# A conv-attention, windowed-attention and expert kernel: the gate projection and the router as one token-major product

## The reference, cut to what matters

```python
# layer 1
t = t + windowed(_ln_t(t), Wp, bp, Wg)      # Wp 128x256, Wg 1x128
t = t + moe(_ln_t(t), router_w, w1, b1, w2, b2)

def windowed(x, Wp, bp, Wg):
    proj = tanh(einsum('btd,ad->bta', x, Wp) + bp)
    g = sigmoid(einsum('bta,oa->bto', proj, Wg))
    return windowed_sum(g * x, 64) / windowed_sum(g, 64)

def moe(tokens, router_w, ...):             # 8 experts, the best 2 of a token
    logits = tokens @ router_w.T
    ...
```

## Time and profile before

| | |
|---|---|
| median of 3 runs | 1453.36 us (1451.39 to 1463.06) |
| the profiled execution, its own time | 1452.11 us |
| its span, first to last instruction | 1450.2 us |
| mean granted TensorE clock | 0.954 of 2.4 GHz |
| busy in the span | PE 90%, DVE 78%, PEld 78%, ACT 68%, POOL 52% |

### The profile page before, as it was taken

One profiled execution on the slowest core, in us unless ns is written; L12 is line 12 of the kernel. 1 busy time (PEld: TensorE's weight loads), 2 busy tenths in 40 slices (PEclk: granted clock), 3 DMA queues, 4 the chain that ended last, 5 costly groups with the idle time before them and its releaser, 6 DMA issues. The chain is left out here.

```text
span 1450.2 us, 29384 instructions
## 1 busy us (share of the span) xinstructions
PE 1300.4 (90%) x8513; PEld 1132.8 (78%) x8513; DVE 1126.9 (78%) x3945; ACT 982.4 (68%) x2090; POOL 761.3 (52%) x964
## 2 busy tenths in 40 slices
PE   3899999989999999999999864999999999999974
PEld 3788878878778878788888743888879899998962
DVE  5478777778878778677778667788879899998972
ACT  1677667666667767667767553777778788888852
POOL 3114655646546565646565447355555556555560
PEclk9999999999999999999999966999999999999995
DMA  8622443535334122222211117766689999999978
GB/s 276 210 81 79 116 117 86 147 78 140 94 91 137 62 75 67 79 67 68 78 46 46 43 48 258 259 227 226 229 262 339 323 343 346 337 342 326 343 261 302
DMA packets 132524, 255.69 MB, mean 176 GB/s; under 512 B 41744, under 2 KB 54800, under 8 KB 132112
## 3 DMA queue, kind: packets, MB, share of 16 engines
q1 hardware_dynamic: 97744, 165.44, 36.2%
q0 software_dynamic: 25920, 71.60, 14.2%
q10 hardware_dynamic: 8704, 16.78, 3.0%
HBM read 120.14 MB, written 100.68 MB: 152 GB/s over the span
## 5 line engine op out<-in xcount | busy, mean ns | idle before, releaser
L1798 POOL DMA_INDIRECT answers<-yy,dest_i x284 | 289.3, 1019 | 223.0 <-DVE yy L1951 123.2
L1521 POOL DMA_INDIRECT sent<-tn,slot_s x256 | 275.9, 1078 | 146.7 <-issue 76.3
L1849 PE MATMUL s_bank<-band,hh 128*128 x568 | 165.8, 292 | 6.0 <-issue 2.9
L1498 POOL TENSOR_TENSOR rs<-ve,halves 128x4 f32<-128x4 f32 x64 | 64.9, 1019 | 195.7 <-DVE ve L1213 195.7
L791 PE MATMUL o_bank<-vv,at 128*128 128x256 f32 x512 | 144.2, 406 | 23.8 <-ACT at L981 14.8
L1849 PE MATMUL s_bank<-w_s,hh 128*128 x568 | 159.1, 280 | 0.5 <-issue 0.5
L1849 PE MATMUL s_bank<-band,hl 128*128 x568 | 158.8, 280 | 0.8 <-issue 0.8
L1933 ACT ACTIVATE zz<-xin 128x256 f32<-128x256 f32 x284 | 147.7, 600 | 10.2 <-issue 6.9
L1899 ACT ACTIVATE hid<-m_bank,b_all 128x512 f32<-128x512 f32 x142 | 93.0, 683 | 86.8 <-remote 60.2
L759 PE MATMUL m_bank<-wvo,band 128*128 128x258 f32 x792 | 135.1, 308 | 13.3 <-DVE band L1351 10.9
L759 PEld LDWEIGHTS m_bank<-wvo,band 128*128 128x128 f32 x792 | 109.5, 195 | 29.4 <-issue 27.7
(11 more groups left out here) (248 smaller groups left out, 3445.2 us busy)
## 6 DMA issues: line engine op xcount, KB each, us to landing
xin<-sent SPq DMA_DIRECT2D x71, 524.0 KB
got<-answers SPq DMA_DIRECT2D x64, 512.0 KB
w1hs<-rT SPq DMA_DIRECT2D x71, 256.0 KB
w1ls<-w_s SPq DMA_DIRECT2D x71, 256.0 KB
xs<-in_x SPq DMA_DIRECT2D x32, 512.0 KB, 8.2
raw<-in_x SPq DMA_DIRECT2D x32, 512.0 KB
out_x<-tn ACTq DMA_DIRECT2D x32, 512.0 KB
answers<-yy,dest_i POOLq DMA_INDIRECT x284
```

What stands on the lines that cost most here:

```text
L1498: eng.tensor_tensor(rs[:, n, :], ve[:, n, :], halves[:, 0, 0:KT], ALU.pow).then_inc(root.sem, 1)
L1521: eng.indirect_dma_start(sent, bass.IndirectOffsetOnAxis(slot_s[:, par, j, k:k + 1], 0), tn[:, par, k, :], None).then_inc(scattered[par], 16)
L1798: eng.indirect_dma_start(answers, bass.IndirectOffsetOnAxis(dest_i[:, at_ % RING, k:k + 1], 0), yy[:, slot, k, :], None).then_inc(rows_out ...
L1849: last = eng.matmul(y_bank[half][:, k * C:(k + 1) * C], hx[:, par, f, ts], rhs, start=(n == 0), stop=(n == 3 * CC - 1))
```

## The change

The router logits are no longer made from the second norm. The token row after the windowed attention is t + w/d, with w the sum of gated, normalized rows xn and d the sum of gates; the first norm's xn has mean zero, so the second norm's mean is the first's, and the router's product on (t - mean) is std * (xn R) + (sum of g * (xn R)) / d. So 8 columns xn R are made once, beside the gate projection, and ride along through the window sums as columns 256 to 263 of `xn1`, `wx` and `tt`.

- The gate projection is now token-major: for each tile `xn1T` is the stationary operand, and the moving one is `wpr`, 128 projection and 8 router columns. A pass with `onesr` and `bpr` puts the bias into the bank (its rounded and its remaining part). Two jobs, `Cp01` and `Cp23`, each with 2 x 136 columns, in place of `Cproj`.
- The product with `wg` is a dot product on VectorE (`dots`), four of 128 elements; `dots` also copies the router columns from the bank to `xn1`, and `routed_part` writes std * (xn R) to `tt`.
- `tokens_turned`, `tokens_taken`, `router` and `gates` are gone, with `tnT` and `logit`. `best_of` searches in `tt`; the difference of the best two is multiplied by the second norm's factor.
- The tanh comes in two halves. `gates_taken` waits for the dots. Banks are dealt out anew; `window(it, 0)` now stands behind the value product 3, and the copy `x_taken(it, 2)` ahead of the gates.

```diff
-        JOBS = ("VV0 AV1 AR0 Epos BX01 AR1 Dtr01 Dtr23 Ctr01 Ctr23 Drouter Cproj AV2 Cgate BX23 AV4 Cwin0 AV3 "
-                "Cwin1 Cwin2 Cwin3").split()
+        JOBS = ("VV0 AV1 AR0 Epos BX01 AR1 Ctr01 Ctr23 Cp01 Cp23 AV2 BX23 AV4 AV3 Cwin0 Cwin1 Cwin2 Cwin3").split()
...
+        bank_of["Cwin3"] = bank_of["Cwin0"]
...
+            eng.tensor_copy(onesr[:, :], ones[:, :])
+            eng.memset(bp_both[:, :, :], 0.0)
+            eng.tensor_copy(bp_high[:, :], bp_rows[:, :]).then_inc(biased, 1)
...
-            def gate_product(it):
-                moved(it, "Ctr01")
-                moved(it, "Ctr23")
-                bank = begin(it, "Cproj")
-                for cc in range(CC):
-                    last = eng.matmul(bank[:, :], wp_s[:, cc, :], xn1T[:, cc, :], start=(cc == 0),
-                                      stop=(cc == CC - 1))
-                end(last, "Cproj")
...
+            def gate_product(it, k0):
+                job = f"Cp{k0}{k0 + 1}"
+                moved(it, f"Ctr{k0}{k0 + 1}")
+                bank = begin(it, job)
+                eng.matmul(bank[:, 0:2 * PR], onesr[:, :], bpr[:, :, :].rearrange(flat), start=True, stop=False)
+                for k in (k0, k0 + 1):
                     for cc in range(CC):
...
+                        last = eng.matmul(bank[:, (k - k0) * PR:(k - k0 + 1) * PR], xn1T[:, cc, k * P:(k + 1) * P],
+                                          wpr[:, cc, :], start=False, stop=(k > k0 and cc == CC - 1))
...
-                if d:
-                    tokens_turned(it, 0)
-                    tokens_turned(it, 2)
...
-                eng.scalar_tensor_tensor(row, m_bank[i][:, 0:C], wden[:, k:k + 1], row, ALU.mult, ALU.add)\
+                eng.scalar_tensor_tensor(row, m_bank[i][:, 0:C + E], wden[:, k:k + 1], row, ALU.mult, ALU.add)\
                    .then_inc(taken[i].sem, 1)
 
+            def dots(it, k0):
+                i = bank_of[f"Cp{k0}{k0 + 1}"]
+                th_ready.wait(eng, it, f"Cth{k0}{k0 + 1}")
...
+                for k in (k0, k0 + 1):
+                    last = eng.tensor_tensor_reduce(out=th[:, k, :], in0=th[:, k, :], in1=wg_rows[:, :], scale=1.0,
+                                                    scalar=0.0, op0=ALU.mult, op1=ALU.add, accum_out=gl[:, k:k + 1])
+                if k0 == 2:
+                    last.then_inc(gate_step.sem, 1)
+                eng.tensor_copy(xn1[:, k0:k0 + 2, C:C + E],
+                                m_bank[i][:, 0:2 * PR].rearrange("p (k n) -> p k n", k=2)[:, :, A:PR])\
+                   .then_inc(taken[i].sem, 1)
+
+            def routed_part(it):
+                for job in ("Cp01", "Cp23"):
+                    taken[bank_of[job]].wait(eng, it, job)
+                done(gate_step, eng.tensor_tensor(tt[:, it.block("C") % TT, :, C:C + E], xn1[:, :, C:C + E],
+                                                  std1[:, :].unsqueeze(2).broadcast_to([P, KT, E]), ALU.mult))
...
+                step(it, route, "Dgap", eng.tensor_tensor(fall[:, :], best[:, :, 1], best[:, :, 0], ALU.subtract))
+                root.wait(eng, it, "Drs2")
+                done(route, eng.tensor_tensor(fall[:, :], fall[:, :], rs[:, 1, :], ALU.mult))
```

More of the change, by code:

```diff
@@ L323, in group_variance @@
                 eng.wait_ge(g_sum, 2)
-            eng.tensor_scalar(g2[:, :], bank[:, 96:96 + CC], EPS, None, ALU.add).then_inc(scale_step, 1)
+            eng.tensor_scalar(g2[:, :], bank[:, 320:320 + CC], EPS, None, ALU.add).then_inc(scale_step, 1)
         def group_root(eng, img, n):
@@ L519, in prologue_vector @@
             eng.tensor_copy(band_prev[:, :], prev_s[:, :])
+            eng.tensor_copy(onesr[:, :], ones[:, :])
+            eng.memset(bp_both[:, :, :], 0.0)
+            eng.tensor_copy(bp_high[:, :], bp_rows[:, :]).then_inc(biased, 1)
+            eng.wait_ge(biased, 1)
+            eng.tensor_tensor(bp_low[:, :], bp_rows[:, :], bp_high[:, :].bitcast(f32), ALU.subtract)\
+               .then_inc(biased, 1)
+            eng.wait_ge(biased, 2)
+            eng.tensor_scalar(bp_low[:, :], bp_low[:, :], ident[:, 1:2], None, ALU.mult).then_inc(biased, 1)
+            eng.wait_ge(biased, 3)
+            for n in range(2):
+                last = eng.scalar_tensor_tensor(bp_both[:, n, 0:A], bp_high[:, :].bitcast(f32), ident[:, 0:1],
+                                                bp_low[:, :], ALU.mult, ALU.add)
+            last.then_inc(biased, 1)
+            eng.wait_ge(biased, 4)
+            eng.tensor_copy(bpr[:, :, :], bp_both[:, :, :])
             eng.tensor_copy(far2[:, 0:REAL].rearrange("p (a b) -> p a b", b=W), far[:, :, 1:W + 1])
@@ L826, in window @@
                 for h in range(2):
-                    last = eng.matmul(bank[:, 0:C + 2], band_cur[:, :], wx[:, par, h, k, :], start=(h == 0),
+                    last = eng.matmul(bank[:, 0:XC], band_cur[:, :], wx[:, par, h, k, :], start=(h == 0),
                                       stop=(alone and h == 1))
@@ L844, in gates @@
-            def gates(it):
-                moved(it, "Cproj")
-                bank = begin(it, "Cgate")
-                for k in range(KT):
-                    last = eng.matmul(bank[:, k:k + 1], pT[:, k * P:(k + 1) * P], wg_s[:, :], start=True,
-                                      stop=True)
-                end(last, "Cgate")
-            def router(it):
-                moved(it, "Dtr01")
-                moved(it, "Dtr23")
-                bank = begin(it, "Drouter")
-                for k in range(KT):
-                    for cc in range(CC):
-                        last = eng.matmul(bank[:, k * E:(k + 1) * E], tnT[:, cc, k * P:(k + 1) * P],
-                                          rw_s[:, cc, :], start=(cc == 0), stop=(cc == CC - 1))
-                for n in range(2):
-                    if image_of(it, 6 - n):
-                        last = group_product(eng, image_of(it, 6 - n), n, bank)
-                end(last, "Drouter")
+            def gate_product(it, k0):
[4 more added lines that the diff above has]
+                for k in (k0, k0 + 1):
+                    for cc in range(CC):
+                        last = eng.matmul(bank[:, (k - k0) * PR:(k - k0 + 1) * PR], xn1T[:, cc, k * P:(k + 1) * P],
+                                          wpr[:, cc, :], start=False, stop=(k > k0 and cc == CC - 1))
+                if k0 == 0:
+                    for n in range(2):
+                        if image_of(it, 6 - n):
+                            last = group_product(eng, image_of(it, 6 - n), n, bank)
+                end(last, job)
@@ L942, in body @@
                 if c:
+                    window(it, 0)
                     window(it, 1)
@@ L1305, in best_of @@
             def best_of(it):
-                i = bank_of["Drouter"]
-                full[i].wait(eng, it, "Drouter")
-                if image_of(it, 6):
-                    group_spread(eng, image_of(it, 6), m_bank[i])
-                if image_of(it, 5):
-                    group_variance(eng, image_of(it, 5), m_bank[i])
-                eng.tensor_copy(logit[:, :, :].rearrange(flat), m_bank[i][:, 0:KT * E])\
-                   .then_inc(taken[i].sem, 1)
-                alone(eng, (taken[i].sem, taken[i].count(it, "Drouter")))
+                scores = tt[:, it.block("D") % TT, :, C:C + E]
                 for k in range(KT):
-                    last = eng.max(best[:, k, :], logit[:, k, :])
+                    last = eng.max(best[:, k, :], scores[:, k, :])
                 last.then_inc(route.sem, 1)
@@ L1431, in body @@
                     band_lower(it)
+                if c:
+                    dots(it, 0)
+                    dots(it, 2)
+                    routed_part(it)
                 if d:
```

124 lines of the change are left out of this document (65 added, 59 removed).

## The result

The changed kernel takes 1483.1 us (median of 4 runs, 1474.2 to 1488.4), the kernel before 1452.4 on the same chip (1449.5 to 1463.1): a ratio of 1.019, 95% interval 1.015 to 1.024. It is slower, by 1.5 to 2.4%, where I had forecast 1419. Both numbers have to be explained.

The account below looks back on a forecast made before the run. TensorE bounds clean rounds now, VectorE (21.8 us a round) after. 1452.1 - 34.5 (rounds) - 3 (hand-over) + 0.5 (start) + 3 (clock) = 1418, with the runs' median 1419 us; range 1403 to 1436.

Parts of the forecast that it names:

- the round after: Walk through one changed round: gates open only 0.4 us earlier, later waits shrink, giving 22.4 us, or 23.15 with statistics.
- the 0.78 wait: VectorE's wait for a window sum in a clean round, 0.78 us, expected to shrink after the change.
- TensorE's lag before the last weighing: TensorE's lateness past the gates, ahead of a round's last weighing; expected to shrink, with no separate size.
- stalls whose cause the trace doesn't name: With the clock, the excess of rounds over 23.95 us, 1.4 in first and 0.7 in later ones; expected to stay.
- The clock: In the thirty rounds, two more low-clock stretches were expected after the change, adding 3 us.
- rival (c): Clock falls in one stretch a round: 22 more stretches give back 40 us, total 1456; chance 0.06.
- (d): Clock falls twice a round, from idleness ahead of fourth value product and third weighing: slower, 1509; chance 0.06.
- stand next to idleness: Claim that today's low-clock stretches in the rounds, some 3.5 us each, lie beside TensorE idle time, such as 3.15 us.
- the hand-over: The 59 us between rounds and expert tiles: search waits and slower router passes go, saving 3 us.
- the sixteen with statistics: Rounds 2 to 17, where VectorE also takes a later image's statistics: 23.15 us each, saving 12.8 together.
- the missing wait at the search: VectorE's 2.03 us wait for the router's product, ahead of the search of the best two experts, goes.
- The idleness ahead of the fourth value product: New TensorE wait for a bank, until the first two dots and their copy are done; no separate size.

Follow-up runs that it names:

- b_same: The kernel before with nothing changed, profiled on a chip without the hold: 1385.8 us (one run).
- a_same: The changed kernel with nothing else changed, on a chip without the hold: 1339.8 us against 1385.1 for the kernel before, 0.966.
- b_split: The kernel before with GpSimd's eight sends of a round issued in two halves of four: 1384.6 us, 0.999 of the kernel before.
- b_nosend: The kernel before with GpSimd's eight indirect sends of a round left out: 1379.8 us, 0.996 of the kernel before.
- b_light: The kernel before without the normalized tokens' transposes and copies, two router passes in place of sixteen, nothing added on VectorE: 1331.8 us, 0.963.
- chip 9: The one experiment chip with the hold; the kernel before takes 1451.6 us there (7 runs).
- b_hold_fill8: b_hold plus eight useless matmuls of 128 columns on TensorE ahead of the fourth weighing, on chip 9: 1495.9 us, 1.031 of the kernel before.
- a_split_6: The changed kernel with a round's eight sends in two halves of four, on chip 9: 1383.0 us (one run), 4.7% less than the kernel before.
- a_hold: The changed kernel with second window sum and last transposed attention read only after all eight sends landed: 1502.1 us, 1.087 of the kernel before.
- b_hold: The kernel before with the same two waits for the sends as a_hold: 1495.7 us, 1.081 of the kernel before.

## Why the prediction was wrong

**The step that failed** is in the round after: "past them the 0.78 wait and TensorE's lag before the last weighing shrink". I had read the 0.78 us ahead of VectorE's window sum as TensorE being late. It was the end of a hold: TensorE starts the last matmul of that sum at 666.95 and its event comes 0.95 us later, not 0.30; the wait isn't there in b_same, and its clean rounds are 23.0 to 23.2 us long, not 23.96. So was, by its place and size, at least part of the "stalls whose cause the trace doesn't name": all 27 jobs that are held for over 2 us lie in rounds of 25.5 us or more. The waits of the kernel before had the sign in them, ten of VectorE ahead of a window sum (total, times, longest), and I didn't ask what "remote" was:

```profile
DVE wden L1288 <- remote: 20.3, 10, 2.7
```

In the changed kernel they didn't shrink: VectorE's wait for the window sum became 1.74 us, and TensorE idles for 1.66 us ahead of the last weighing, behind a wait of 3.24 of ScalarE. It is not that it puts more of TensorE's work into the sends: between 3 and 10 us after a round's first send it starts 7.6 jobs a round, the kernel before 8.1. The hold sets in earlier. Of the jobs in that stretch that can be paired 128 of 172 take over 0.8 us in the changed kernel, 44 of 150 in the kernel before. Why is open.

The account in the rounds, hold against no hold: +42.5 us for the kernel before, +116.6 for the changed one. The difference of 74.1 takes up the gain of 45.4 and leaves the loss of 28.7. The sum of the prediction has no term for it.

**The clock** was sized at 3 us. TensorE is busy for 43 us more in the changed kernel's rounds than a_same is with the same instructions, against 9 before: 34 us, near rival (c), which put 40 on it. It stands not where (c) and (d) had it, ahead of the fourth value product and the third weighing, but mostly at the window sums and in a few rounds at the fourth weighing, and it is the hold's follower: in a_same's rounds the clock is 1.00.

The prediction also has it that today's low stretches "stand next to idleness". Of the eight in the kernel before's rounds (a ninth runs into the hand-over) only four do, with pieces of 1.2 to 3.2 us. The other four begin right behind the router's sixteen passes of 8 columns, with no idle piece of over 0.13 us within 8 us. One of them, to be read beside the earlier trace rows, where the same three groups take 1.92, 1.11 and 1.88:

```profile
729.05 1.92 PE L858 MATMUL m_bank<-rw_s,tnT 128*128 128x8 f32 x16
730.83 1.91 PE L791 MATMUL o_bank<-vv,at 128*128 128x256 f32 x4
732.54 2.81 PE L840 MATMUL m_bank<-xn1T,wp_s 128*128 128x512 f32 x4
```

In b_same all five low stretches within the rounds lie there, in b_split all seven, in b_nosend five of six (I leave out the one that runs into the hand-over). a_same, without the router's passes, and b_light, with two in place of sixteen, have none in their rounds. So the change takes a part of the clock's loss away, which the prediction counted as staying.

In a_same TensorE also idles ahead of the weighings, 34.5 us in thirty rounds, in pieces of 0.25 and of 0.73 to 0.83 in the late ones and of 0.95 in the early ones, and its clock is 1.00. By the rule that I had quoted from the Trainium skill ("TensorE: Matmul & The Clock Gate", section "A second HAM failure mode: psum-queue depth-cycling") small idle times between groups would have been enough; these traces don't bear it out for pieces of under 1 us. My own reading in the prediction, that only idle times near 2 us and above count, doesn't hold either: the changed kernel's clock falls behind pieces of 1.3 us, that of the kernel before without any, and in a_same one of 2.09 us ahead of 748.80 has no fall within 9 us of it.

**What held**, on the chips without the hold. Clean rounds save 1.8 to 1.9 us (23.2 to 21.35), forecast 1.55; the last fourteen rounds together 31.5, forecast 21.7; the sixteen with statistics 13.9, forecast 12.8. Of the 31.5 some 8 are the clock, by my estimate: b_same has its five low stretches in these fourteen rounds, and two of these rounds take 24.7 us where their neighbours take 23.2. A clean late round is 21.1 to 21.4 us and not 22.4, mostly because its base was 23.2 and not 23.95. The whole is 0.966, forecast 0.976. TensorE's 20.3 us busy, the missing wait at the search, dots of 0.29 with a read of 0.08, passes of 136 columns at 0.105 (0.84 for eight), are right or near; the bias pass takes 0.2 to 0.3 where I had 0.15. The idleness ahead of the fourth value product is nearly absent; that ahead of the third weighing is 0.7 to 0.8, half of what I wrote. The hand-over gave 4.2 in place of 3, the start nothing. The expert tiles, left out of the sum, lost 8.2, where the hold acts too; that this part differs between two kernels with the same code there I can't derive (83 of their jobs are held for over 2 us, against 72).

**The rivals.** None of mine was the case. (d) had the right sign and, in the clock, a part of the mechanism; but it put all of the loss on the clock, and most of it is waiting. A rival "completions come late while the sends run" should have stood there, with the row of remote waits.

**Open.** Why some chips hold TensorE's semaphore events during a series of indirect DMAs and others don't (of five chips in the experiments one does); why the hold sets in at the third send in some rounds and at the eighth in others, and earlier in the changed kernel; and that the chip of the first comparison is like chip 9 is inferred from the kernel before's time and from the holds in the trace of b_hold_fill8, not known. Neither kernel was run without sends on a chip with the hold, the unchanged changed kernel wasn't run on chip 9, and a_split_6 is one run: that the series of sends makes the hold rests on the events' times and on that run.

## What to carry to other kernels

A wait whose releaser was long done, or that the profile calls remote, is not the releaser's lag: look at what GpSimd and the DMA queues do in that stretch before you count it as something that a faster engine takes away. A gain on one engine is only worth what lies behind the last fixed event of a round; put the same fixed wait into both kernels, as in a_hold and b_hold, and see whether anything is left. Compare on more than one chip: this change is 1.9% slower on one and 3.4% faster on another, and with four sends at a time, 0.8% dearer than eight where nothing is held, it beat the kernel before on both kinds. And a clock loss that an average of 0.98 shows may lie in narrow passes, not in idle time: find its stretches before you price it.

## What the runs showed of the hardware

- On one kind of chip (kernel before 1452 us) TensorE's semaphore events are held during a series of 1 us indirect DMAs of GpSimd, for up to 6.6 us in the rounds and 7.1 in the expert tiles, and come in a burst as the last send lands; on four others (1382 to 1386 us) with the same code the longest is 0.65.
- On a chip without the hold the sends are almost free: left out altogether, with GpSimd busy for 260 to 279 us less, they give the kernel before 0.4% and the changed one nothing (0.966 with and without).
- 13 useless matmuls in an idle place of each round made a kernel 41 us faster (1502 to 1461, on two chips on which the kernel before takes 1382 and 1386); the granted clock in its rounds went from 0.92 and 0.90 to 0.99 and 1.00.
- TensorE's clock can fall without idle time: in b_same five times in fourteen rounds, each time right behind sixteen passes of 8 columns, with TensorE busy; two of these rounds took 24.7 us where their neighbours took 23.2.
